# Causal attention on one core: scores of two steps, then products of the preceding two

## The chip, the cores and the metric

The kernel runs on one core of a Trainium2 chip. Its engines work side by side, each through a queue of its own in program order, and meet only at semaphores: TensorE (PE, matrix products into the eight banks of PSUM), VectorE (DVE), ScalarE (ACT), GpSimd (POOL), and the DMA queues, of which this kernel uses SyncE's (SP). The metric is the device time of one execution in microseconds (us); less is better.

## The reference, cut to what matters

The whole model is two layers, each a token mixer and a feed-forward part, on 2 sequences of 1024 tokens with 512 channels. The change lies in the attention of the second layer, which has 16 heads of 32 channels:

```python
qkv = x @ qkv_w.T + qkv_b
q, k = _rope(q), _rope(k)
scores = jnp.einsum('bhqd,bhkd->bhqk', q, k) / np.sqrt(D)
scores = jnp.where(causal, scores, -jnp.inf)
attn = jax.nn.softmax(scores, axis=-1)
out = jnp.einsum('bhqk,bhkd->bqhd', attn, v).reshape(b, t, c)
return out @ out_w.T + out_b
```

## The kernel before, in words

`attend` (L1858) works through 8 units; a unit is 4 heads of one sequence. For each unit there are `NS` = 12 steps. A step (`STEPS`, L1865) is one pair of a block of 512 queries (`qc`) and a tile of 128 keys (`j`): steps 0 to 3 belong to the first block of queries, steps 4 to 11 to the second. Steps 0 to 3 and 8 to 11 lie on the diagonal; there the columns left of it are left out, so that their widths are 512, 384, 256 and 128 columns. Steps 4 to 7 are 512 wide.

For one step, for each of 4 heads, TensorE computes the transposed scores (`scores`, L2039, 98 rows of the array by 128 columns) into one of `ST` = 3 PSUM banks `st`; ScalarE takes the exponential out of the bank into `pt` (`exps`, L2009); GpSimd masks the diagonal (L1991). Then TensorE multiplies `pt` by the values into `num` and by ones into `den` (`pv`, L2058: eight matmuls a step, four beside each other, each in 32 columns of the array). `num` and `den` are one bank each, and gather over all steps of one block of queries; after the last step of a block (`ENDS`: 3 and 11) they are copied out, and DVE inverts the denominators in 4 chunks (`invert`, L2084) and multiplies (L2087); SP stores the result.

The softmax needs each query's maximum. `Maxima` computes it one unit ahead: 48 score pieces per unit (`piece`, L1372, up to 512 columns, three PSUM banks `mx` in turn), each reduced by DVE (`top`: L1384 with the mask, or L1387). The pieces of a head come in groups of four, with widths 128, 256, 384, 512; 512, 128, 512, 256; 512, 384, 512, 512. `pieces_at` says which pieces stand with which step: they are put between the step's four score matmuls. With `LAST_PIECES` = 8 and `FRONT` = 12, steps 0 to 8 carry 36 pieces (4 each) of the next unit and steps 10 and 11 carry 12 pieces (6 each) of the one after it. At `TURN_STEP` = 9 the maxima are joined (L1392), transposed by TensorE (L1397), negated by ACT (L1402) and DVE (L1407), and sent by SP as two more rows of the queries. The third piece that follows waits for that negation, since it writes the bank of the transpose.

The order is written out by hand, in one loop for each engine. TensorE issues the scores of step g (with pieces), then `pv` of step g - 2 (`LAG` = 2); `pt` has `PT` = 3 buffers. ACT issues the exponentials of step g and, where step g - 2 ended a block, then the copies of `den` and `num` (`copy_out`, L2000 and L2001). DVE issues the pieces of step g, and after them one chunk of inversion at steps 2 to 5 (second block of the unit before) and 7 to 10 (first block of this unit). The last unit (7) has no pieces; there ACT also splits the attention output of earlier units into high parts (`out.high`, L1811, two tiles at each of steps 6 to 9) and DVE into low parts. At step 4 of each unit GpSimd's queue has three casts of expert weights (`narrow`, L2175), which wait for their loads by SP's queue; the loads stand behind those of the next queries and keys, which wait for the last `pv` of the unit before.

## Time and profile before

| | us |
|---|---|
| median of 3 runs | 1529.63 |
| lowest and highest of these | 1527.41 and 1530.99 |
| span of the profiled execution (first to last instruction) | 1527.3 |
| TensorE busy in it | 1465.1 (96%) |
| VectorE busy | 976.4 (64%) |
| ScalarE busy | 614.1 (40%) |
| GpSimd busy | 472.3 (31%) |
| attention, first score matmul to the first matmul of the output projection | 905.91 to 1245.68 |

The page names only the span for the profiled execution; the runs' median lies 2.3 us above it. Busy times of TensorE overlap: matmuls are pipelined, and the end of each is modelled, so that gaps on TensorE are read from the starts of its rows. "Idle before" in a row of the timeline is the engine's idle time, with what ended it.

### The profile page before, as it was taken

Reading aid. Unit: us, or ns where it says so; the run is one execution under the profiler, and the core shown is the slowest. Engines: PE = TensorE matmul, PEld = TensorE weight load, DVE = VectorE, ACT = ScalarE, POOL = GpSimd, SP = SyncE. Lnnn points to the kernel's source line nnn. Section 1 sums busy time; section 2 is a strip of 40 time slices with the busy share of each in tenths; the row PEclk is TensorE's granted clock in tenths of the full one; section 3 lists DMA queues with packets and bytes.
Section 4 is the critical chain, followed back from the end, with each engine's and each line's share of the span. In section 5 each row is a group of like instructions: output and inputs, shape, how many; then the busy total and the mean of one; then the engine's idle time right before and its main releaser. Section 6 shows DMA issues by size and latency. Waiting matters only on the chain. (4 is left out here: it accounts for less than half of the span.)

```text
span 1527.3 us, 22410 instructions
## 1 busy us (share of the span) xinstructions
PE 1465.1 (96%) x7681; PEld 1072.6 (70%) x7696; DVE 976.4 (64%) x1897; ACT 614.1 (40%) x1079; POOL 472.3 (31%) x391
## 2 busy tenths in 40 slices
PE   7999989999999999999999999999999999999987
PEld 5788778788888888888888774444444458777554
DVE  6888987854545554454233666778787557667664
ACT  4343455613421441342121124555554546432544
POOL 1233334303420440241152231211223237103773
PEclk9999999999999999999999989999999999999999
DMA  6121347504320430334256685666556445853336
GB/s 215 34 71 65 152 166 248 180 14 138 96 69 29 151 96 27 110 96 149 82 191 192 207 244 138 192 198 155 155 173 213 150 152 218 303 208 132 105 101 238
DMA packets 105228, 223.38 MB, mean 146 GB/s; under 512 B 9328, under 2 KB 35312, under 8 KB 104240
## 3 DMA queue, kind: packets, MB, share of 16 engines
q1 hardware_dynamic: 101392, 211.96, 42.8%
q0 software_dynamic: 3744, 10.23, 2.2%
q8 instruction: 54, 0.88, 0.2%
q14 instruction: 38, 0.31, 0.1%
HBM read 157.54 MB, written 64.36 MB: 145 GB/s over the span
## 5 line engine op out<-in xcount | busy, mean ns | idle before, releaser
L2009 ACT ACTIVATE at_pt<-at_st 128x512 f32<-128x512 f32 (+3 forms) x384 | 164.1, 499 | 147.4 <-PE at_st L2039 146.5
L969 POOL TENSOR_TENSOR ff_w_lo<-ff_raw,ff_w_hi 128x1024 fp32r<-128x1024 f32 x64 | 153.7, 2402 | 220.8 <-ACT ff_w_hi L999 206.6
L115 PE MATMUL op_bank<-ff_x_hi,ff_w_lo 128*128 128x512 f32 x512 | 199.9, 390 | 0.2 <-issue 0.2
L116 PE MATMUL op_bank<-ff_x_lo,ff_w_hi 128*128 128x512 f32 x512 | 199.6, 390 | 0.0
L117 PE MATMUL op_bank<-ff_x_hi,ff_w_hi 128*128 128x512 f32 x512 | 199.5, 390 | 0.0
L1239 DVE TENSOR_TENSOR ff_h_lo<-ff_hf,ff_h_hi 128x512 f32 (+1 forms) x64 | 146.8, 2293 | 53.9 <-ACT ff_h_hi L1127 53.6
L999 ACT ACTIVATE ff_w_hi<-ff_raw 128x1024 fp32r<-128x1024 f32 x64 | 67.9, 1063 | 118.3 <-PE op_bank L117 116.0
L2039 PE MATMUL at_st<-mx_qp,mx_kp 98*128 98x512 f32 (+3 forms) x288 | 103.0, 390 | 12.6 <-ACT at_pt L2009 9.5
L1384 DVE CUSTOM_DVE_ANT_0 mx_mx<-mx_mx,mx_mask 128x128 f32<-128x128 f32 (+2 forms) x200 | 101.5, 517 | 21.1 <-PE mx_mx L1372 20.0
L115 PEld LDWEIGHTS op_bank<-ff_x_hi,ff_w_lo 128*128 128x128 f32 x512 | 96.4, 188 | 20.7 <-issue 0.6
L117 PEld LDWEIGHTS op_bank<-ff_x_hi,ff_w_hi 128*128 128x128 f32 x512 | 96.4, 188 | 20.4
L116 PEld LDWEIGHTS op_bank<-ff_x_lo,ff_w_hi 128*128 128x128 f32 x512 | 96.4, 188 | 20.1
L2039 PEld LDWEIGHTS at_st<-mx_qp,mx_kp 98*128 98x128 f32 x288 | 54.3, 195 | 69.7 <-issue 33.4
L115 PE MATMUL mx_mx<-ff_down_hi,ff_h_lo 128*128 128x512 f32 x256 | 100.2, 391 | 0.0
L116 PE MATMUL mx_mx<-ff_down_lo,ff_h_hi 128*128 128x512 f32 x256 | 99.7, 389 | 0.0
L117 PE MATMUL mx_mx<-ff_down_hi,ff_h_hi 128*128 128x512 f32 x256 | 99.7, 389 | 0.0
L1231 DVE SCALAR_TENSOR_TENSOR ff_hf<-op_bank,ff_sc,ff_hf 128x512 f32<-128x512 f32 x64 | 48.0, 750 | 72.3 <-PE op_bank L117 71.6
L1991 POOL TENSOR_SCALAR_AFFINE_SELECT at_pt<-at_pt 128x512 f32<-128x512 f32 x64 | 41.1, 646 | 149.9 <-ACT at_pt L2009 149.8
L1372 PE MATMUL mx_mx<-mx_kp,mx_qp 96*128 96x512 f32 (+1 forms) x208 | 75.9, 371 | 6.7 <-DVE mx_tops L1384 2.9
L2058 PE MATMUL at_den<-at_pt,at_ones 128*32 128x512 f32 (+3 forms) x768 | 82.2, 500 | 0.0
L1120 ACT ACTIVATE ff_hf<-op_bank,ff_sc 128x512 f32<-128x512 f32 x64 | 44.2, 690 | 82.6 <-PE op_bank L117 82.6
L1565 POOL TENSOR_TENSOR qkv_part_lo<-qkv_whole,qkv_part_hi 128x512 fp32r<-128x512 f32 x32 | 42.6, 1332 | 88.3 <-ACT qkv_part_hi L1580 80.8
(467 smaller groups left out, 3333.4 us busy)
## 6 DMA issues: line engine op xcount, KB each, us to landing
ff_raw<-in_Wug SPq DMA_DIRECT2D x64, 512.0 KB, 3.6
at_raw<-in_expert_gu SPq DMA_DIRECT2D x16, 704.0 KB, 12.1
mx_qp<-q_hi SPq DMA_DIRECT2D x12, 512.0 KB, 6.5
mx_kp<-k_hi SPq DMA_DIRECT2D x12, 512.0 KB, 11.6
at_raw<-in_expert_d SPq DMA_DIRECT2D x8, 768.0 KB, 13.7
expert_gu_bf<-at_cast SPq DMA_DIRECT2D x16, 352.0 KB, 10.9
ex_e_gu<-expert_gu_bf SPq DMA_DIRECT2D x8, 704.0 KB, 8.3
tm_ln_res<-in_x SPq DMA_DIRECT2D x4, 1024.0 KB, 5.5
```

The source lines that it names most:

```text
L115: pe.matmul(out, cut_l(ll), cut_r(rh), start=first, stop=False, **kw)
L116: pe.matmul(out, cut_l(lh), cut_r(rl), start=False, stop=False, **kw)
L117: return pe.matmul(out, cut_l(lh), cut_r(rh), start=False, stop=last, **kw)
L969: pool.tensor_tensor(w[j][1][:, :, :, :], raw[:, j], f32(w[j][0][:, :, :, :]), ALU.subtract)\
L999: act.activation(w[j][0][:, :, :, :], raw[:, j], ACT.Copy).then_inc(w_hi_ready, 1)
L1231: dve.scalar_tensor_tensor(hf[:, j, :], up[j][:, :], sc[:, UP, bass.ds(n + j, 1)], hf[:, j, :], ALU.mult, ALU.mult).then_inc(hf_ready, 1)
L1239: dve.tensor_tensor(h_lo[:, bass.ds(n + j, 1), :], hf[:, j:j + 1, :], f32(h_hi[:, bass.ds(n + j, 1), :]), ALU.subtract).then_inc(h_lo_read ...
L1372: pe.matmul(bank[:, 0:hi - lo], self.qp[j][0:R_MAX, h, qt * P:(qt + 1) * P], self.kp[j][0:R_MAX, h, lo:hi], start=True, stop=True).then_in ...
L1384: dve.tensor_tensor_reduce(piece, piece, self.mask[:, TB - (hi - lo):], 1.0, -3e38, ALU.add, ALU.max, out)\
L2009: act.activation(pt[:, s % PT, h, off:TB], st[(s * HG + h) % ST][:, off:TB], ACT.Exp, scale=SCALE).then_inc(exp_done, 1)
L2039: pe.matmul(st[(s * HG + h) % ST][:, off:TB], kp[j][0:ROWS, h, kt * P:(kt + 1) * P], qp[j][0:ROWS, h, qc * TB + off:(qc + 1) * TB], start= ...
L2058: mm = pe.matmul(total[rows, off:TB], vv[u % SLOTS][:, kt, rows] if lhs is None else lhs[:, :], pt[:, s % PT, h, off:TB], start=first, sto ...
```

## The change

The loops of TensorE, ACT and DVE go by pairs of steps (`PAIR` = 2). TensorE issues the scores of two steps with their pieces, then `pv` of the two steps before. `pt` has 4 buffers in place of 3. The pieces are spread anew: `TURN_STEP` = 9 is now also the last step of the first stretch and `FRONT` is 8, so that every step of a middle unit carries 4 pieces. ACT copies the denominators only, behind the exponentials of the next pair; DVE copies the numerators (`copy_num`), behind its pieces and inversions of that pair. DVE inverts two chunks in a pair: in the pairs (2, 3) and (4, 5) for the unit before, in (6, 7) and (8, 9) for this unit. ACT waits at the start for the stores of the values by the stage before (`v_stored`), and DVE does in unit 0 before pair (2, 3). `last_at`, where later rows of the residual lie, moves by one buffer.

```diff
@@ -1865,20 +1865,19 @@
     STEPS = [(qc, j) for qc in range(QC) for j in range((qc + 1) * TT)]
     NS = len(STEPS)
     DIAGS = sum(j >= qc * TT for qc, j in STEPS)
-    LAST_PIECES, TURN_STEP, FRONT = 8, 9, 12
-    LAG = 2
-    PT = LAG + 1
+    PAIR = 2
+    TURN_STEP, FRONT = 9, 8
+    PT = 2 * PAIR
     ST = 3
     DIVIDE_CHUNKS = 4
     CHUNK = TB // DIVIDE_CHUNKS
-    DIVIDE_LAST, DIVIDE_FIRST = 2, 7
     OW_STEP, SPLITS = 1, {6: [(0, (0, 1))], 7: [(0, (2, 3))], 8: [(1, (0, 1))], 9: [(1, (2, 3))]}
-    assert NS % PT == 0 and NS * HG % ST == 0 and NP % 3 == 0 and QC == 2 and (UNITS - 2) % SLOTS == 0
+    assert NS % PAIR == 0 and NS * HG % ST == 0 and NP % 3 == 0 and QC == 2 and (UNITS - 2) % SLOTS == 0
     with Bench(nc, "at_") as b:
         mx.add_slot(b)
         qp, kp, vv = mx.qp, mx.kp, mx.vv
         pt = b.sb("pt", [P, PT, HG, TB])
-        last_at = b.next_at() - 2 * TT * C * 4
+        last_at = b.next_at() - 3 * TT * C * 4
         num_sb, den_sb = b.sb("num_sb", [P, QC, TB]), b.sb("den_sb", [P, QC, TB])
         ones = b.sb("ones", [P, HD])
         st = [b.psum(f"st{s}", [P, TB]) for s in range(ST)]
@@ -1910,20 +1909,27 @@
 
         def pieces_at(u, s):
 
-            if s <= LAST_PIECES:
+            if s <= TURN_STEP:
                 begin = FRONT if u else 0
                 count = NP - begin
-                lo, hi = (begin + count * n // (LAST_PIECES + 1) for n in (s, s + 1))
+                lo, hi = (begin + count * n // (TURN_STEP + 1) for n in (s, s + 1))
                 return [(u + 1, n) for n in range(lo, hi)] if u + 1 < UNITS else []
-            if s <= TURN_STEP or u + 2 >= UNITS:
+            if u + 2 >= UNITS:
                 return []
             after = NS - 1 - TURN_STEP
             lo, hi = (FRONT * n // after for n in (s - TURN_STEP - 1, s - TURN_STEP))
             return [(u + 2, n) for n in range(lo, hi)]
 
-        def place(g):
-
-            return g // NS, g % NS
+        def pairs():
+
+            return [(u, [s, s + 1]) for u in range(UNITS) for s in range(0, NS, PAIR)]
+
+        def ended_before(u, steps):
+
+            s = steps[0] - 1
+            if s in ENDS:
+                return u, ENDS.index(s)
+            return (u - 1, QC - 1) if s < 0 and u else None
 
         @block.sync
         def _(sp):
@@ -1994,33 +2000,34 @@
 
         @block.scalar
         def _(act):
-            def copy_out(u, qc):
+            def copy_den(u, qc):
                 act.wait_ge(pv_done, u * NS + ENDS[qc] + 1)
                 at_least(act, o_stored[qc], u * DMA)
                 act.activation(den_sb[:, qc, :], den[:, :], ACT.Copy).then_inc(copied, 1)
-                act.activation(num_sb[:, qc, :], num[:, :], ACT.Copy).then_inc(copied, 1)
 
             def exps(u, s):
                 off = diag(s) or 0
 
-                at_least(act, pv_done, u * NS + s - LAG)
+                at_least(act, pv_done, u * NS + s - PT + 1)
                 for h in range(HG):
                     act.wait_ge(scores_done, (u * NS + s) * HG + h + 1)
                     act.activation(pt[:, s % PT, h, off:TB], st[(s * HG + h) % ST][:, off:TB], ACT.Exp,
                                    scale=SCALE).then_inc(exp_done, 1)
 
-            for g in range(UNITS * NS):
-                u, s = place(g)
-                exps(u, s)
-                if g >= LAG and place(g - LAG)[1] in ENDS:
-                    ended, at = place(g - LAG)
-                    copy_out(ended, ENDS.index(at))
-                if s == TURN_STEP and u + 1 < UNITS:
+            for stored in mx.v_stored:
+                act.wait_ge(stored, NB * TT // 2 * DMA)
+            for u, steps in pairs():
+                for s in steps:
+                    exps(u, s)
+                    if u == UNITS - 1:
+                        for i, ks in SPLITS.get(s, ()):
+                            out.high(act, i, ks, pv_done)
+                ended = ended_before(u, steps)
+                if ended:
+                    copy_den(*ended)
+                if TURN_STEP in steps and u + 1 < UNITS:
                     mx.negate_high(act, u + 1)
-                if u == UNITS - 1:
-                    for i, ks in SPLITS.get(s, ()):
-                        out.high(act, i, ks, pv_done)
-            copy_out(UNITS - 1, QC - 1)
+            copy_den(UNITS - 1, QC - 1)
             out.high(act, 2, range(KT), pv_done)
             out.scale(act, 0)
             out.high(act, 3, range(KT), pv_done)
@@ -2060,18 +2067,21 @@
                 mm.then_inc(pv_done, 1)
 
             pe.wait_ge(ones_small_set, 1)
-            for g in range(UNITS * NS):
-                u, s = place(g)
-                if s == 0:
+            before = None
+            for u, steps in pairs():
+                if steps[0] == 0:
                     pe.wait_ge(mx.ones_set, min(u + 1, SLOTS))
                     pe.wait_ge(mx.rows_loaded, (u + 1) * 2 * DMA)
-                scores(u, s)
-                if g >= LAG:
-                    pv(*place(g - LAG))
-                if s == TURN_STEP and u + 1 < UNITS:
+                for s in steps:
+                    scores(u, s)
+                if before:
+                    for s in before[1]:
+                        pv(before[0], s)
+                if TURN_STEP in steps and u + 1 < UNITS:
                     mx.turn(pe, u + 1)
-            for g in range(UNITS * NS - LAG, UNITS * NS):
-                pv(*place(g))
+                before = u, steps
+            for s in before[1]:
+                pv(before[0], s)
             for i in range(NB - 1):
                 out.project(pe, i)
             expert_tensor(pe)
@@ -2086,23 +2096,43 @@
                     dve.wait_ge(inverted, (u * QC + qc + 1) * DIVIDE_CHUNKS)
                     dve.tensor_tensor(num_sb[:, qc, :], num_sb[:, qc, :], den_sb[:, qc, :], ALU.mult).then_inc(divided, 1)
 
-            for g in range(UNITS * NS):
-                u, s = place(g)
-                for of, n in pieces_at(u, s):
-                    mx.top(dve, of, n)
-                if s == LAST_PIECES and u + 1 < UNITS:
+            def copy_num(u, qc):
+                dve.wait_ge(pv_done, u * NS + ENDS[qc] + 1)
+                at_least(dve, o_stored[qc], u * DMA)
+                dve.tensor_copy(num_sb[:, qc, :], num[:, :]).then_inc(copied, 1)
+
+            for u, steps in pairs():
+                if u == 0 and steps[0] == PAIR:
+                    for stored in mx.v_stored:
+                        dve.wait_ge(stored, NB * TT // 2 * DMA)
+                for s in steps:
+                    for of, n in pieces_at(u, s):
+                        mx.top(dve, of, n)
+                    if u == UNITS - 1:
+                        if s == OW_STEP:
+                            ow.low(dve)
+                        for i, ks in SPLITS.get(s, ()):
+                            out.low(dve, i, ks)
+                if TURN_STEP in steps and u + 1 < UNITS:
                     mx.join(dve, u + 1)
-                if s == TURN_STEP and u + 1 < UNITS:
+                if u and steps[0] == PAIR:
+                    invert(u - 1, 1, 0)
+                    invert(u - 1, 1, 1)
+                if u and steps[0] == 2 * PAIR:
+                    invert(u - 1, 1, 2)
+                    invert(u - 1, 1, 3)
+                if steps[0] == 3 * PAIR:
+                    invert(u, 0, 0)
+                    invert(u, 0, 1)
+                if steps[0] == 4 * PAIR:
+                    invert(u, 0, 2)
+                    invert(u, 0, 3)
+                ended = ended_before(u, steps)
+                if ended:
+                    copy_num(*ended)
+                if TURN_STEP in steps and u + 1 < UNITS:
                     mx.negate_low(dve, u + 1)
-                if u and 0 <= s - DIVIDE_LAST < DIVIDE_CHUNKS:
-                    invert(u - 1, 1, s - DIVIDE_LAST)
-                if u == UNITS - 1:
-                    if s == OW_STEP:
-                        ow.low(dve)
-                    for i, ks in SPLITS.get(s, ()):
-                        out.low(dve, i, ks)
-                if 0 <= s - DIVIDE_FIRST < DIVIDE_CHUNKS:
-                    invert(u, 0, s - DIVIDE_FIRST)
+            copy_num(UNITS - 1, QC - 1)
             for chunk in range(DIVIDE_CHUNKS):
                 invert(UNITS - 1, 1, chunk)
             out.add(dve, 0)
```

## Rows read from the trace of the kernel before

**Rows 1.** The page: its first line.
```profile
span 1527.3 us, 22410 instructions
```
**Rows 2.** Windows: us, busy (x count) of PE, PEld, DVE, ACT, POOL, PEclk, DMA share, GB/s.
```profile
990.00:995.00 5.00, 4.87 (x22) 1.80 (x23) 3.91 (x13) 0.43 (x3) 1.35 (x3) 0.68 0.06 20
```
**Rows 3.** TensorE's timeline, steps 7 and 8 of a unit: start, duration, engine, line, operation.
```profile
1064.84 0.40 PE L2039 MATMUL at_st<-mx_qp,mx_kp 98*128 98x512 f32 x1
1065.08 0.28 PE L1372 MATMUL at_mx<-mx_kp,mx_qp 96*128 96x256 f32 x1
1065.29 1.06 PE L2058 MATMUL at_num<-at_pt,mx_vv 128*32 128x512 f32 x8
1066.17 1.04 PE L2058 MATMUL at_den<-at_pt,at_ones 128*32 128x512 f32 x8
1067.14 0.50 PE L2039 MATMUL at_st<-mx_qp,mx_kp 98*128 98x512 f32 x1
1067.48 0.40 PE L1372 MATMUL mx_mx<-mx_kp,mx_qp 96*128 96x512 f32 x1
```
**Rows 4.** TensorE's timeline: first scores of steps 7, 10, 0, 2, 4, 6, 7.
```profile
1063.44 0.50 PE L2039 MATMUL at_st<-mx_qp,mx_kp 98*128 98x512 f32 x1
...
1074.37 0.36 PE L2039 MATMUL at_st<-mx_qp,mx_kp 98*128 98x256 f32 x1
...
1083.68 0.50 PE L2039 MATMUL at_st<-mx_qp,mx_kp 98*128 98x512 f32 x1
...
1088.95 0.38 PE L2039 MATMUL at_st<-mx_qp,mx_kp 98*128 98x256 f32 x1
...
1095.64 0.50 PE L2039 MATMUL at_st<-mx_qp,mx_kp 98*128 98x512 f32 x1
...
1101.06 0.50 PE L2039 MATMUL at_st<-mx_qp,mx_kp 98*128 98x512 f32 x1
...
1105.80 0.50 PE L2039 MATMUL at_st<-mx_qp,mx_kp 98*128 98x512 f32 x1
```
**Rows 5.** TensorE's timeline: pieces 3 and 4 of step 10.
```profile
1075.33 0.41 PE L1372 MATMUL mx_mx<-at_kp,at_qp 96*128 96x384 f32 x1 [0.24 <-issue]
...
1076.39 0.50 PE L1372 MATMUL mx_mx<-at_kp,at_qp 96*128 96x512 f32 x1 [0.54 <-DVE mx_tops L1384]
```
**Rows 6.** DVE's timeline: pieces, an inversion, the product.
```profile
1064.83 0.29 DVE L1384 CUSTOM_DVE_ANT_0 mx_mx<-mx_mx,mx_mask 128x128 f32<-128x128 f32 x1
...
1065.99 0.95 DVE L2084 RECIPROCAL at_den_sb<-at_den_sb 128x128 f32<-128x128 f32 x1
1067.92 0.69 DVE L1387 TENSOR_REDUCE mx_tops<-mx_mx 128x1 f32<-128x512 f32 x1 [0.98 <-PE mx_mx L1372]
1068.53 0.56 DVE L1384 CUSTOM_DVE_ANT_0 mx_mx<-mx_mx,mx_mask 128x384 f32<-128x384 f32 x1
...
1102.51 0.69 DVE L2087 TENSOR_TENSOR at_num_sb<-at_num_sb,at_den_sb 128x512 f32<-128x512 f32 x1
```
**Rows 7.** ACT's timeline: four exponentials; the denominators' copy; two splits of the last unit.
```profile
1064.04 2.07 ACT L2009 ACTIVATE at_pt<-at_st 128x512 f32<-128x512 f32 x4 [2.16 <-PE at_st L2039]
...
1089.08 0.60 ACT L2000 ACTIVATE at_den_sb<-at_den 128x512 f32<-128x512 f32 x1 [0.30 <-PE at_den L2058]
...
1231.01 1.17 ACT L1811 ACTIVATE at_o_hi<-at_raw_o 128x512 fp32r<-128x512 f32 x2
```
**Rows 8.** GpSimd's timeline: the last cast of a unit and the first masks behind it.
```profile
1074.43 1.47 POOL L2175 CAST at_cast<-at_raw 128x1536 bf16<-128x1536 f32 x1 [1.40 <-DMA at_raw<-in_expert_d]
1075.85 1.22 POOL L1991 TENSOR_SCALAR_AFFINE_SELECT at_pt<-at_pt 128x512 f32<-128x512 f32 x2
```
**Rows 9.** SP's timeline: its first load of the stage, behind its wait for the values' stores.
```profile
905.91 0.38 SPq L1715 DMA_DIRECT2D ow_raw<-in_outT  x1
```
**Rows 10.** TensorE's timeline: step 0 of the last unit, which has no pieces.
```profile
1208.46 0.96 PE L2039 MATMUL at_st<-mx_qp,mx_kp 98*128 98x512 f32 x3
1209.71 0.50 PE L2039 MATMUL at_st<-mx_qp,mx_kp 98*128 98x512 f32 x1 [0.29 <-ACT at_pt L2009]
```

## The prediction, made before the change was run

> **What bounds the kernel now.** I read the page's engines and slices first: TensorE is busy nearly everywhere, so the question is what its time in the attention is made of. Then TensorE's timeline of one unit, from start to start, since the ends of pipelined matmuls are modelled; then the timelines of DVE, ACT, GpSimd and SP over the same unit, to see which of them each gap waits for; last the granted clock by stretches of 5 us. The span is 1527.3 us [rows 1], and a unit in the middle takes 1105.80 - 1063.44 = 42.36 us [rows 4].
>
> Three things fill a unit. First the matmuls: within a stretch of scores and pieces a 512-column matmul follows the other after 0.24 us, a product of a step (eight matmuls, four at a time) takes 0.88 us for `num` and as much for `den` [rows 3]. Second the switch between the two kinds. The 256-column piece at 1065.08 should take half of 0.24 and the product starts 0.21 later: 0.09 lost. From `den` to the next score there are 0.97 instead of 0.88 (0.09), and from that score to the next matmul 0.34 instead of 0.24 (0.10) [rows 3]. That is 0.28 us for each step, whoever waits for whom. Third the waits for DVE and ACT: in step 10, piece 3 comes 0.96 us after the first score (the negation), and piece 4 stands idle 0.54 us for DVE [rows 4, 5]. TensorE is on the path throughout; ACT and DVE reach it through the three banks each that they must empty.
>
> **The change part by part.** *Switches.* One for two steps instead of one for each: 6 of 12 go, 6 x 0.28 = 1.7 us a unit, 13 us over 8 units. No other engine covers them, so this gain is sure; the question is how much of it waits give back.
>
> *The stretch of scores in a pair.* It holds 8 scores and 8 pieces. TensorE alone would need 8 x 0.24 for 512-wide scores, 0.6 to 0.9 us for each four pieces (by their columns), and 0.19 for the switch. Two limits stand against that. Score k waits for exponential k - 3: the first exponential starts 0.60 after the first score and takes 0.6, and four take 2.07, one in 0.5 [rows 3, 4, 7]; so the fourth score comes at 1.25 (as 1209.71 - 1208.46 in the unit without pieces [rows 10]) and the eighth at 1.25 + 4 x 0.52 = 3.3. Piece k waits until DVE has read piece k - 3. DVE starts 0.44 after a 512-column piece (1067.92 against 1067.48 [rows 3, 6]) and goes on every 0.61 for 512 columns (1067.92 to 1068.53), and by duration less 0.08 every 0.48 for 384 and 0.21 for 128, about 0.34 for 256 [rows 6]: 1.7, 1.8 and 2.3 us for the three groups of four. A read is visible to TensorE some 0.2 us after the next one begins, my estimate from such rows.
>
> *DVE's other work.* An inversion takes 0.95, or 0.82 until the next can start (estimate: 0.95 less the overlap that pieces show), the product 0.69 [rows 6]. New is the copy of 128x512 from PSUM: no row shows it; the nearest, the reduction of a bank, is 0.69 (next start 0.61), ACT's copy of such a bank 0.60 [rows 6, 7]. I take 0.61 and 0.5 to 1.0 as bounds. ACT in turn loses a copy of such a size, twice a unit; it was not on the path except behind the end of a block. The VectorE: DVE Perf Modes page of the Trainium skill (Specifications) puts VectorE nearer to SBUF and ScalarE nearer to PSUM, which speaks against moving a PSUM copy to DVE; the two rows differ by 0.09 us, so by them it is worth 0.2 us a unit at most.
>
> *Pair by pair, middle units* (before, from [rows 4]; after = scores stretch + products of the pair before, 0.09 less for their inner border; products in proportion to columns):
> - (0, 1): before 5.27. DVE's eight reads run from 0.78; piece 7 needs the read of piece 4 at 3.5; stretch 4.08, products 1.41: 5.49.
> - (2, 3): before 6.69. The narrow scores leave TensorE little to do, and DVE copies the numerators until 0.74 first; piece 7 waits until 3.28; stretch 3.71, products 3.17: 6.88.
> - (4, 5): before 5.42. The eighth score, at 3.3, decides; 3.75 + 1.41 = 5.16. DVE is through with its pieces at 4.4, but has two inversions and the product (2.4) still, and only then the copy.
> - (6, 7): before 4.74 + 3.70 = 8.44 (steps 7 and 8 from the unit before). That copy ends 2.2 us after the pair begins, with three pieces waiting in their banks: piece 3 comes at 3.0 instead of 1.4; stretch 5.57, products 3.61: 9.18.
> - (8, 9): before 7.23. DVE is free again; 3.83 + 3.67 (with the transpose) = 7.50.
> - (10, 11): before 9.31, with 12 pieces, two inversions and a product on DVE between them. Now 8 pieces and nothing else; the negation still holds piece 3 until 0.96. Stretch 3.6, products 3.17: 6.77.
>
> The sum is 40.98: 1.38 less than 42.36. Five units (1 to 5) give -6.9. Unit 6 prepares no unit after it, so it has no pieces in (10, 11) before or after; without that pair it loses, 34.2 against 33.05: +1.2. Unit 0 has no inversions of a unit before it, so that its pairs keep up; it gains the 2.5 us of (10, 11) and five switches, 1.4: -3.9, with 2 us either way, as its pieces are spread differently. Unit 7 has no pieces, and a pair of 512-wide steps needs 3.3 + 0.43 for its scores against 2 x 1.68 before; the two splits in ACT's queue between exponentials (1.17 for two [rows 7]) now hold the eighth score in pairs (6, 7) and (8, 9), by 0.7 and 1.4: +2.4 in all.
>
> *Waits added, and moved queues.* ACT's wait for the values' stores comes first in its queue, ahead of all exponentials; SP waits for the same semaphores and had its load out at 905.91 [rows 9], before the first score ended: 0 us, and 0.5 if it is seen later. DVE's stands behind the pieces of a whole pair: 0. The fourth `pt` buffer lets exponentials run two steps ahead; only products free it, earlier than needed. SP's loads hang on the last product of the unit before, which moves with the unit. GpSimd's casts end at 1075.9 [rows 8]. The last product before that unit's loads ended about 1046.7 (the next unit's is done by 1089.08 [rows 7], and a unit takes 42.36): 29.2 us. Masks 8 and 9 follow 0.6 and 1.2 us later: 35.4 us after the unit's start. The first product that needs mask 8 starts at 37.8, so the casts are hidden by some 2.4 us; they are a floor if everything else goes better. The end of the stage moves as a whole: the projection that follows starts on blocks loaded long before.
>
> Sum: -6.9 - 3.9 + 1.2 + 2.4 = -7.2 us. The profiled execution would have a span of 1520.1; the median stands 2.3 us above the span of before, so 1522.4.
>
> **The rivals.**
> *A, DVE keeps up.* The waits of (2, 3) and (6, 7) are smaller than drawn (1.2 and 2.0 us above what TensorE needs), for instance as reads are seen earlier. Then the casts become the floor: 2.4 us less in each of units 1 to 5, 1510. For it: DVE is idle for a fifth of the new unit (4 x 5.8 for pieces, 8 x 0.82, 2 x 1.3, some 33 us of 41). Against it: the copy is bound to the last product, whatever its size.
>
> *B, the clock.* In 990 to 995 the granted clock was 0.68 [rows 2], a part of that stretch at 1.2 instead of 2.4 GHz; it cost 0.32 x 5 = 1.6 us, and the timeline shows the like once more in a later unit, at the same place: behind step 10, whose waits are those of rows 5, in two units of seven. The new stretch of (6, 7) idles 2.0 us of 5.57, and (10, 11) 1.4 of 3.6. If the clock fell once in each of units 0 to 6, that were 5 x 1.6 = 8 us more: 1530. The page TensorE: Matmul & The Clock Gate of the Trainium skill (Why this matters for your kernels) says that idle gaps between bursts of matmuls bring the clock down; by it alone waits as short as those drawn keep the clock, and the sum stays 1522, while by the row it can fall behind several waits of 0.54 us at most.
>
> *C, waits that take turns (slower).* A matmul after a wait is followed only 0.34 us later, as after a switch (rows 3; 0.10 each time). If in each pair the scores wait for ACT and the pieces for DVE alternately, 10 of 16 matmuls pay that, some 0.6 us a pair more than I counted, 3.6 a unit in units 0 to 6 at most: 1548; at half of it, 1535. From 0.2 us a pair on the gain is gone. For it: both limits lie within 0.3 us of each other in (0, 1), (4, 5) and (8, 9). Against it: three banks on each side let one wait cover the other.
>
> *D, the switch stays.* If the 0.28 us belong to the first matmuls behind a semaphore and not to the change of kind, then pairs save none of it: +13, 1536. Against it: inside a product, from `num` to `den`, nothing is lost.
>
> **How the numbers follow.** Forecast 0.47 (its own range 1515 to 1529), A 0.15, B 0.16, C 0.16, D 0.06. A measurement of this kernel can tell 0.2%, 3.1 us, from no change. Faster by more: most of the forecast and A, 0.57. Within: B and the forecast's upper edge, 0.21. Slower: C and D, 0.22. For 8 in 10 the range runs from A to the half of C, with 2 us on either side: 1508 to 1537.
>
> **What would show it.** A middle unit of 41 us, with (10, 11) shortest against before (6.8 for 9.3) and (6, 7) longer (9.2 for 8.4), its fourth piece waiting for DVE behind a numerators' copy that starts 1.6 us late. One switch of 0.28 a pair. In unit 7, the eighth scores of (6, 7) and (8, 9) waiting for ACT behind a split. Wrong would be: products that wait for masks (A's floor), a clock under 1.0 in more than two units (B), or waits for ACT and DVE alternating through a stretch (C).

## The result, and the profile after

The median rose from 1529.73 to 1533.41 us (16 runs each; one of before took 4622.33 us, and without it before's median is 1529.63): a ratio of 1.0026, with a 95% interval of 1.0017 to 1.0036. The kernel became slower by a quarter of a per cent, where the prediction had 1522.4 and "faster" as the likeliest; its range, 1508 to 1537, held the time.

The page of after, its first line, the engines' busy times and the granted clock by slices of the span (before: [rows 1]):

```profile
span 1531.1 us, 22440 instructions
...
PE 1473.1 (96%) x7696; PEld 1079.4 (70%) x7696; DVE 983.6 (64%) x1913; ACT 603.6 (39%) x1063; POOL 474.7 (31%) x391
...
PEclk9999999999999999999999989999999999999999
```

In tenths of full speed the clock looks the same as before. As a mean over the span it is 0.980, and before it was 0.989. Over the runs of after the time goes with this mean: 1528.56 us at 0.984, 1533.29 at 0.980, 1538.38 at 0.978.

By windows of 5 us the loss has places. Columns as in [rows 2]; these are the ends of pair (10, 11) of unit 1 and of pair (6, 7) of unit 3:

```profile
985.00:990.00 5.00, 4.57 (x23) 2.38 (x27) 3.70 (x15) 1.58 (x6) 2.28 (x4) 0.76 0.17 61
990.00:995.00 5.00, 5.00 (x35) 2.48 (x27) 1.59 (x4) 1.77 (x4) 0.00 (x0) 0.90 0.00 0
...
1055.00:1060.00 5.00, 3.81 (x15) 2.45 (x14) 4.90 (x13) 3.87 (x8) 0.00 (x0) 0.93 1.05 213
1060.00:1065.00 5.00, 5.00 (x35) 1.25 (x33) 3.00 (x6) 0.63 (x2) 0.00 (x0) 0.73 1.06 399
```

The last column but two is the granted clock. Each window's length times what its clock lacks to 1, summed from 905 to 1250, is 22.1 us after against 10.3 before. The first 15 us of the stage hold 5.1 (after) and 6.8 (before) of it; the rest is 17.0 against 3.5. The span grew by 3.8, which less the clock's 11.8 leaves -8.0. That is near the forecast of -7.2, and the clock took it back. The sum is rough: it prices every window as if TensorE's clock alone set its length.

A "fall" is a stretch of time at the lower clock. How one looks on TensorE, in pair (6, 7) of unit 3 (start, duration, engine, line, operation, idle before):

```profile
1054.63 0.50 PE L2046 MATMUL at_st<-mx_qp,mx_kp 98*128 98x512 f32 x1
...
1056.09 0.39 PE L2046 MATMUL at_st<-mx_qp,mx_kp 98*128 98x512 f32 x1
1057.62 0.50 PE L1372 MATMUL mx_mx<-mx_kp,mx_qp 96*128 96x512 f32 x1 [1.14 <-DVE mx_tops L1387]
...
1059.36 0.69 PE L1372 MATMUL mx_mx<-mx_kp,mx_qp 96*128 96x384 f32 x1
...
1060.83 1.94 PE L2065 MATMUL at_num<-at_pt,mx_vv 128*32 128x512 f32 x8
1062.54 1.10 PE L2065 MATMUL at_den<-at_pt,at_ones 128*32 128x512 f32 x8
```

The pair begins at 1054.63; piece 3 is next behind the score of 1056.09, and TensorE stands idle for 1.14 us before it. From about 1059.4 matmuls take 0.63 to 0.69 instead of 0.34 to 0.40, and a product of eight starts 1.71 before the next instead of 0.88 [rows 3]: TensorE is at 1.2 GHz until 1062.5. What piece 3 waited for stands in DVE's timeline:

```profile
1053.88 1.76 DVE L2094 RECIPROCAL at_den_sb<-at_den_sb 128x128 f32<-128x128 f32 x2
1055.67 0.69 DVE L2097 TENSOR_TENSOR at_num_sb<-at_num_sb,at_den_sb 128x512 f32<-128x512 f32 x1
1056.28 0.68 DVE L2102 COPY at_num_sb<-at_num 128x512 f32<-128x512 f32 x1
1056.88 0.68 DVE L1387 TENSOR_REDUCE mx_tops<-mx_mx 128x1 f32<-128x512 f32 x1
```

Two inversions, the product and the new copy of pair (4, 5) run until 2.25 us after pair (6, 7) has begun; only then, at 1056.88, does DVE read the first of three full banks.

A second thing was in no step of the prediction. In unit 1, at the border of pairs (8, 9) and (10, 11):

```profile
982.92 1.47 POOL L2205 CAST at_cast<-at_raw 128x1536 bf16<-128x1536 f32 x1 [1.43 <-DMA at_raw<-in_expert_d]
983.26 1.66 DVE L2097 TENSOR_TENSOR at_num_sb<-at_num_sb,at_den_sb 128x512 f32<-128x512 f32 x1
...
984.85 0.27 DVE L1407 SCALAR_TENSOR_TENSOR mx_neg_lo<-mx_mx,mx_neg_hi 32x128 fp32r<-32x128 f32 x1
...
985.22 0.41 PE L1372 MATMUL mx_mx<-mx_kp,mx_qp 96*128 96x384 f32 x1 [0.66 <-issue]
```

DVE's product takes 1.66 us instead of 0.69 [rows 6], and ends half a microsecond behind GpSimd's cast. The negation stands behind it, and piece 3 comes 1.49 us after the pair's first score (983.73), where 0.96 was counted. (10, 11) has 4.32 and 4.37 for 3.60 in the two units with the longest products, 1 and 5. Before, that product came 3.5 to 3.8 us after the end of the third cast, and in units 0 to 6 all products took 0.69.

In unit 2, where (10, 11) took longest (4.58), the same cast met another operation of DVE, the join of the maxima; the last row is the join of unit 3, which met none:

```profile
1025.73 1.47 POOL L2205 CAST at_cast<-at_raw 128x1536 bf16<-128x1536 f32 x1 [1.43 <-DMA at_raw<-in_expert_d]
1025.81 1.42 DVE L1392 TENSOR_TENSOR mx_tops<-mx_tops 128x16 f32<-128x16 f32 x1
...
1070.29 0.17 DVE L1392 TENSOR_TENSOR mx_tops<-mx_tops 128x16 f32<-128x16 f32 x1
```

The inversions, the product and the negation stand behind the join, and piece 3 of unit 2 comes 1.75 us after the pair's first score.

The lengths of the units in us, from first score to first score of (0, 1), unit 7 to the first matmul of the projection, before and after: unit 0 49.16 and 44.73; units 1 to 5 together 214.80 and 216.68; unit 6 38.59 and 40.91; unit 7 37.22 and 41.45.

### The profile page after: what moved, and what is told of

Its sections match the earlier page's. It is cut to its first block and busy times, and to the rows that moved or that the text cites. A ratio compares the mean times of both kernels' runs of the same rounds, so it can differ in the third digit from the quotient of the medians.

```text
span 1531.1 us, 22440 instructions
## 1 busy us (share of the span) xinstructions
PE 1473.1 (96%) x7696; PEld 1079.4 (70%) x7696; DVE 983.6 (64%) x1913; ACT 603.6 (39%) x1063; POOL 474.7 (31%) x391
## 5 line engine op out<-in xcount | busy, mean ns | idle before, releaser
L2205 POOL CAST at_cast<-at_raw 128x1408 bf16<-128x1408 f32 (+1 forms) x24 | 33.4, 1394 | 123.4 <-DMA at_raw<-in_expert_gu 114.4
```

## The experiments

"After" is the changed kernel. Stretches are from first score to first product, products from there to the next score, in us. Medians are of four to ten runs; rows, stretches and falls are those of the one profiled execution of each kernel.

**The inversions one pair later.** DVE's inversions of the pairs (4, 5), (6, 7) and (8, 9), and the products behind them, are moved one pair on in units 0 to 6; nothing else.

```diff
+                late = PAIR if u + 1 < UNITS else 0
-                if u and steps[0] == 2 * PAIR:
+                if u and steps[0] == 2 * PAIR + late:
                     invert(u - 1, 1, 2) ...
-                if steps[0] == 3 * PAIR:
+                if steps[0] == 3 * PAIR + late:
                     invert(u, 0, 0) ...
-                if steps[0] == 4 * PAIR:
+                if steps[0] == 4 * PAIR + late:
                     invert(u, 0, 2) ...
```

> The changed kernel with the inversions of units 0 to 6 moved by one pair: those of pair (4, 5) to (6, 7), those of (6, 7) to (8, 9), those of (8, 9) to (10, 11), where DVE had nothing beside pieces; unit 7 as before the move. Theory: DVE is through with the pieces of (4, 5) before the products end, so its copy starts at once, and the first piece of (6, 7) is read at 0.75 us instead of 2.2: the stretch takes 4.1 instead of 5.55 to 6.2 us, with no wait long enough to bring the clock down; 1.5 to 2 us a unit for the wait and some 1.2 for the clock: 1510 to 1518. Rival (the order in pairs as such lets the clock fall): the stretch shrinks, the products after it still run at half clock in about each unit: 1522 to 1525.

Measured 1512.03 us, ratio to before 0.9886 (0.9864 to 0.9908): faster than both kernels. Pair (6, 7) of unit 3 now, on TensorE and DVE:

```profile
1047.07 0.50 PE L2046 MATMUL at_st<-mx_qp,mx_kp 98*128 98x512 f32 x1
...
1048.51 0.40 PE L2046 MATMUL at_st<-mx_qp,mx_kp 98*128 98x512 f32 x1
1048.75 0.40 PE L1372 MATMUL mx_mx<-mx_kp,mx_qp 96*128 96x512 f32 x1
...
1051.16 1.07 PE L2065 MATMUL at_num<-at_pt,mx_vv 128*32 128x512 f32 x8
...
1047.20 0.69 DVE L2102 COPY at_num_sb<-at_num 128x512 f32<-128x512 f32 x1 [0.74 <-PE at_den L2065]
```

The copy starts 0.13 after the pair (1047.07), as soon as the denominators' last matmul ends, and piece 3 stands nowhere. The stretch is 4.09 instead of 5.5 to 6.2, the units 1 to 5 are 39.21 to 39.24 long, and in them the clock never falls. The casts no longer meet a product (all 0.69 in units 0 to 6). This one edit takes away the wait of (6, 7) and the meeting with the cast together; the next runs take them one by one.

**Matmuls in place of the wait.** In after, the fourth score matmul of step 6 is issued seven times in units 1 to 6, where piece 3 would wait. It adds work and takes no wait away.

```diff
+                    if s == 3 * PAIR and h == HG - 1 and 0 < u < UNITS - 1:
+                        for _ in range(6):
+                            pe.matmul(st[(s * HG + h) % ST][:, off:TB], ...)
                     pe.matmul(st[(s * HG + h) % ST][:, off:TB], ...)
```

> The changed kernel, in which TensorE fills its wait for DVE in pair (6, 7) of units 1 to 6: the fourth score matmul of step 6 is issued seven times instead of once, with the same result each time (1.4 us more matmuls in a wait of 1.1 to 1.6 us). Nothing else changes. Theory (the clock falls because TensorE idles in that stretch): the stretch keeps its 5.55 us, since DVE sets it, the clock stays up behind it, and the products take 3.57 instead of 4.4 to 4.8 us: 4 to 8 us less than the changed kernel, 1526 to 1529, although work was added. Rival (the clock falls for something else, such as the kind of matmul or the time since the last fall): falls stay, and the time is the same or up to 3 us longer, 1533 to 1537.

Measured 1526.31, 0.9992 of before (0.9976 to 1.0008): 7 us less than after by the medians, 5 by the ratios to before. Unit 3:

```profile
1053.35 1.54 PE L2048 MATMUL at_st<-mx_qp,mx_kp 98*128 98x512 f32 x6
...
1054.96 0.44 PE L1372 MATMUL mx_mx<-mx_kp,mx_qp 96*128 96x512 f32 x1
...
1057.48 1.06 PE L2069 MATMUL at_num<-at_pt,mx_vv 128*32 128x512 f32 x8
```

Piece 3 comes 3.06 us after the pair began (1051.90), as late as without the fill (2.99), and the stretch is 5.55 to 5.58; but in units 1 to 6 the products behind it take 3.57 throughout, where four of the six had 4.46 to 4.84. Piece 3 comes no earlier, so what (6, 7) gained came from the clock alone. It is not the whole gain. Units 1 to 5 are 10.0 us shorter together, 4.7 of it at (6, 7) and 5.3 at (10, 11), which the fill does not touch: one fall there in place of four. Why is not shown.

**The last product away from the cast.** In after, only DVE's fourth inversion of the first block and its product go from pair (8, 9) to (10, 11), behind the negation.

```diff
                 if steps[0] == 4 * PAIR:
                     invert(u, 0, 2)
-                    invert(u, 0, 3)
+                if steps[0] == 5 * PAIR:
+                    invert(u, 0, 3)
```

> The kernel after, with one thing moved: DVE's last inversion of the first block and the product behind it, from the pair (8, 9) to the pair (10, 11), behind the negation. In the trace of after that product took 1.66, 1.14 and 1.71 us in units 1, 3 and 5 where it overlapped GpSimd's third cast of 1.47 us, against 0.69 without such an overlap, and the negation stands behind it. Theory (two causes, this one and the wait in (6, 7)): the product is 0.69 again, the stretch (10, 11) 3.6 in all units where it was up to 4.58, so -2.5 us over the units, and the clock no longer falls behind (10, 11), where products took 4.42 to 4.84 for 3.14 in four units, -6.1; (6, 7) stays at 5.5 with its own falls: 1523 to 1528. Rival 1 (the overlap costs nothing on the path): 1531 to 1535. Rival 2 (the product is all that the kernel with later inversions gained by): 1510 to 1515.

Measured 1522.64, ratio 0.9953 (0.9936 to 0.9970), a little under the theory of two causes. The cast's row, the negation and piece 3, and further on the product:

```profile
984.38 1.47 POOL L2206 CAST at_cast<-at_raw 128x1536 bf16<-128x1536 f32 x1 [1.44 <-DMA at_raw<-in_expert_d]
...
985.72 0.28 DVE L1407 SCALAR_TENSOR_TENSOR mx_neg_lo<-mx_mx,mx_neg_hi 32x128 fp32r<-32x128 f32 x1 [1.89 <-ACT mx_neg_hi L1402]
986.10 0.41 PE L1372 MATMUL mx_mx<-mx_kp,mx_qp 96*128 96x384 f32 x1
...
990.42 0.69 DVE L2097 TENSOR_TENSOR at_num_sb<-at_num_sb,at_den_sb 128x512 f32<-128x512 f32 x1
```

Piece 3 comes 0.96 after the first score (985.14), (10, 11) takes 3.60 in all units, and three units measure 40.66 to 40.71. One point was not expected: (6, 7) still takes 5.55, yet its products are slow in one unit of six, not four. Of the 9.9 us that units 1 to 5 gain, 6.9 come at (10, 11) and 3.1 at (6, 7). And the clock falls once behind a (10, 11) of 3.60.

**ACT copies again.** After, with the numerators' copies back on ACT.

```diff
                 act.activation(den_sb[:, qc, :], den[:, :], ACT.Copy).then_inc(copied, 1)
+                act.activation(num_sb[:, qc, :], num[:, :], ACT.Copy).then_inc(copied, 1)
...
-                if ended:
-                    copy_num(*ended)
```

> The changed kernel with one part undone: ACT copies the numerators again, behind the denominators; the pairs, the spread of pieces and the places of the inversions stay. Theory (the clock falls behind the stretch of scores of pair (6, 7), in which TensorE waits for DVE, whose queue is late by two inversions, the product and the copy): DVE starts the pieces of (6, 7) 0.6 us earlier, so that stretch shrinks from 5.55 or more to about 4.95 us in units 1 to 6, and the clock falls more seldom there, but not never: 3 to 8 us less than the changed kernel, 1526 to 1530. Rival (the copy on DVE is the whole trouble): the stretch comes down to some 4.2 us and the clock stays up, 1518 or less. Rival (the clock falls for the order in pairs as such): the stretch shrinks, but the clock falls as often: 4 us less, 1529.

Measured 1531.09, ratio 1.0023 (1.0003 to 1.0043), with 10 runs from 1525.25 to 1540.85: no clear gain, and above the theory's 1526 to 1530. The trace, of a run of 1528.14, says why: (6, 7) shrinks from 5.54 to 4.96 and its products are fast in units 1 to 6, but DVE, early by the copy's time, now meets the cast with its product in each of the units 1 to 5:

```profile
1026.76 1.47 POOL L2202 CAST at_cast<-at_raw 128x1536 bf16<-128x1536 f32 x1 [1.43 <-DMA at_raw<-in_expert_d]
1027.07 1.70 DVE L2098 TENSOR_TENSOR at_num_sb<-at_num_sb,at_den_sb 128x512 f32<-128x512 f32 x1
...
1029.07 0.41 PE L1372 MATMUL mx_mx<-mx_kp,mx_qp 96*128 96x384 f32 x1 [1.06 <-issue]
```

(10, 11) takes 4.54 to 5.07 for it. TensorE stands idle there for 1.06 to 1.59 us in one piece, and yet the products behind are slow in one unit of the five only (4.84 for 3.14).

**DVE's copies alone.** The kernel before, with nothing of the change but the numerators' copies on DVE, behind its inversion of the step.

```diff
-                act.activation(num_sb[:, qc, :], num[:, :], ACT.Copy).then_inc(copied, 1)
...
                     invert(u, 0, s - DIVIDE_FIRST)
+                if g >= LAG and place(g - LAG)[1] in ENDS:
+                    ended, at = place(g - LAG)
+                    copy_num(ended, ENDS.index(at))
```

> The kernel before with one part of the change alone: DVE copies the numerators, behind the pieces and the inversion of the step; ACT copies the denominators only. Order by single steps, as before. Theory (DVE is the engine that is late at step 6): the stretch of step 6, which waits for DVE before the change, grows by some 0.6 us in units 0 to 6, and ACT's exponentials of steps 2 and 6 start 0.5 us earlier for 0.3 us of gain at step 2: +2 to +5 us, 1532 to 1535, with the clock falling no more often than before. Rival (the copy is hidden on DVE): 1528 to 1530.

Measured 1535.68, ratio 1.0054 (1.0037 to 1.0070), a little over the theory's upper end. Step 6 of unit 3:

```profile
1060.56 0.68 DVE L2091 COPY at_num_sb<-at_num 128x512 f32<-128x512 f32 x1
...
1061.56 0.60 PE L1372 MATMUL mx_mx<-mx_kp,mx_qp 96*128 96x512 f32 x1 [1.29 <-DVE mx_tops L1384]
...
1062.09 1.94 PE L2057 MATMUL at_num<-at_pt,mx_vv 128*32 128x512 f32 x8
```

Behind an inversion and a product, the copy makes TensorE wait 1.29 us in one piece; step 6 has 3.6 for 2.9, and its products take 3.37 for 1.85 in five of the units 1 to 6. Unit 3 becomes 44.39 for 42.39 long, three quarters of that by the clock. The theory had the clock fall no more often than before; that part of it failed.

**The new spread alone.** The kernel before, with four pieces at each step and none in groups of six.

```diff
-    LAST_PIECES, TURN_STEP, FRONT = 8, 9, 12
+    LAST_PIECES, TURN_STEP, FRONT = 9, 9, 8
```

> The kernel before, with the new spread of pieces alone (four with each of the steps 0 to 9 and 10, 11, none in groups of six); no pairs, copies by ACT. Theory: the gain forecast for (10, 11) belongs to the spread and not to the pairs: eight pieces there for twelve, 4 x 0.53 us less for DVE, which is on the path there, and four pieces more in step 9, +0.6; -1.5 us in each of six units: 1518 to 1522. Rival (the spread needs the pairs: step 9's pieces now hold the transpose and the negation up by as much): 1527 to 1532.

Measured 1521.71, ratio 0.9944 (0.9923 to 0.9964). Units 2 and 3 are 41.07 and 41.12 long, 1.27 less; steps 10 and 11 with their products have 7.44 for 9.31, and step 9's scores 1.89 for 1.46. No pair is needed for this part. In units 1, 4 and 5 the join meets the third cast and takes 1.42, 1.27 and 1.42, TensorE waits for it, and step 9's products last 2.66 to 2.81 for 1.89: the spread alone can bring about this collision.

**Pairs on TensorE alone.** The kernel with later inversions, TensorE going by single steps again.

```diff
-                for s in steps:
-                    scores(u, s)
-                if before:
-                    for s in before[1]:
-                        pv(before[0], s)
+                for n, s in enumerate(steps):
+                    scores(u, s)
+                    if before:
+                        pv(before[0], before[1][n])
```

> The kernel with later inversions (1512.0), with all as it is on the other engines, but TensorE going by single steps again: scores of one step, products of one step. It undoes the part of the change that the prediction called a sure gain. Theory 1 (the prediction's): six switches of 0.28 us come back in each unit and nothing else changes, 8 x 1.7 = +13 us: 1525. Theory 2 (the switches saved were paid back by waits in the doubled stretch at once): the rows of before for steps with four pieces sum to 5.27 + 6.71 + 5.43 + 7.22 = 24.63 us for (0, 1), (2, 3), (4, 5), (8, 9), and the kernel with later inversions has 5.47 + 6.80 + 5.19 + 7.34 = 24.80 for the same: 1508 to 1515.

Measured 1518.36, ratio 0.9922 (0.9905 to 0.9939), between the two theories. A switch and its rows, to be held against [rows 3]:

```profile
1082.54 0.38 PE L1372 MATMUL at_mx<-at_kp,at_qp 96*128 96x256 f32 x1
1082.85 1.06 PE L2065 MATMUL at_num<-at_pt,mx_vv 128*32 128x512 f32 x8
1083.73 1.04 PE L2065 MATMUL at_den<-at_pt,at_ones 128*32 128x512 f32 x8
1084.70 0.33 PE L2046 MATMUL at_st<-mx_qp,mx_kp 98*128 98x128 f32 x1
```

Again 0.97 from `den` to the next score. Units 1 to 5 are 41.35 to 41.38 long against 39.21 to 39.24: 2.14 us for six switches, 0.80 of it in the products, the rest in the scores with their waits, among them one of 0.56 for DVE in step 0. The total rose by 6.3 only, since unit 7 loses its wait for the splits (next run) and the clock lost less at the start of the stage (5.1 us for 7.5; below).

**The splits behind both exponentials.** The kernel with later inversions; in unit 7 ACT's splits follow the pair's eight exponentials.

```diff
                 for s in steps:
                     exps(u, s)
+                for s in steps:
                     if u == UNITS - 1:
                         for i, ks in SPLITS.get(s, ()):
```

> The kernel with later inversions (1512.0), and in the last unit ACT's splits behind both exponentials of a pair instead of between them. Theory: the eighth score waits for ACT no longer; (6, 7) 4.99 to 3.7, (8, 9) 4.50 to 3.7, and the products behind (6, 7) 6.36 to 3.57 as the clock stays: -4.9 us, 1507. Rival (ACT's time comes back in the next pair, whose exponentials then wait behind two splits): 1511 to 1513.

Measured 1506.83, ratio 0.9853 (0.9837 to 0.9870), the best of all. In after, pair (6, 7) of unit 7 has a split on ACT between exponentials, and the eighth score behind it:

```profile
1225.40 1.18 ACT L1811 ACTIVATE at_o_hi<-at_raw_o 128x512 fp32r<-128x512 f32 x2
...
1227.12 0.80 PE L2046 MATMUL at_st<-mx_qp,mx_kp 98*128 98x512 f32 x1 [1.01 <-ACT at_pt L2014]
```

Here eight exponentials run in one go, and the split follows beside the products:

```profile
1202.03 4.02 ACT L2014 ACTIVATE at_pt<-at_st 128x512 f32<-128x512 f32 x8
...
1202.67 2.46 PE L2047 MATMUL at_st<-mx_qp,mx_kp 98*128 98x512 f32 x5 [0.31 <-ACT at_pt L2014]
...
1205.84 0.72 ACT L1811 ACTIVATE at_o_hi<-at_raw_o 128x512 fp32r<-128x512 f32 x1
```

(6, 7) takes 3.67 for 4.99 and (8, 9) 3.47 for 4.50. The clock still falls behind (6, 7), where scores wait up to 0.31 us for ACT; the products have 5.24 for 6.37, where the theory had 3.57. The stretches went as the theory said; that the median met it (1507) is in part luck.

**ACT copies in the balanced kernel.** The run above, with the edit of "ACT copies again".

> The best kernel so far (1506.8), with ACT copying the numerators again: it undoes DVE's copies where DVE's work is spread evenly. Theory (a copy costs little on either engine where neither is late; the copy by DVE hurt only behind the inversions of (4, 5)): 1505 to 1509, with stretches that move by 0.2 us at most. Rival 1 (DVE is the limit still, and each copy by it costs 0.6 us): 2 x 0.6 us in each of seven units less, 1498 to 1500. Rival 2 (ACT's copies hold up the exponentials of the next pair): 1510 to 1515.

Measured 1510.99, ratio 0.9884 (0.9867 to 0.9902): slower by 4 us than with DVE's copies, outside the theory and in the range of the second rival. In unit 3 the exponentials of (6, 7) start 1.10 us after its first score instead of 0.64, behind ACT's two copies, and the fourth score waits for them, as that rival had it. (6, 7) has 4.38 to 4.40 for 4.09 in units 1 to 6 and 4.16 for 3.67 in unit 7, whose (2, 3) has 2.84 for 2.35, with a fall behind it; the other stretches of units 1 to 6 stay within 0.02. Here, where DVE is not late, its copy is the cheaper one.

**The clock at the start of the stage.** Ahead of the first score TensorE idles 3.1 us in every kernel so far, and the granted clock of 905 to 910 is 0.50 to 0.70 behind that. From 910 to 920 it differs: 0.50 with the splits behind, 0.75 and 0.66 in after, 0.96 and 1.00 with ACT's copies in the balanced kernel. So the "about 0.5 for 15 us" that the next expectation gives for every kernel is wrong. To the kernel with the splits behind, twelve matmuls are added before the attention's first wait:

```diff
+            for _ in range(12):
+                pe.matmul(mx.bank[1][:, :], mx.qp[0][0:R_MAX, 0, 0:P], mx.kp[0][0:R_MAX, 0, 0:TB], ...)
             pe.wait_ge(ones_small_set, 1)
```

> The best kernel so far (later inversions and splits behind, 1506.8), and before the attention's first wait twelve matmuls of 512 columns more into a bank that nothing reads, in the 3.1 us in which TensorE waits there for GpSimd's ones. In every kernel so far that wait is followed by a granted clock of about 0.5 for 15 us (905 to 920). Nothing else changes and work is added, so this tests the clock alone. Theory (an idle TensorE brings the clock down, and the lower clock costs what the rows at either level say): the first two stretches of scores take about 4.0 + 3.7 for 11.8 and the first products 3.14 for 5.2, -6 us: 1500 to 1502; with the clock kept only in part, 1503 to 1505. Rival (the first stretches are bound by DVE and ACT at either clock, or the clock falls for another reason): 1506 to 1509.

Measured 1512.10, ratio 0.9902 (0.9879 to 0.9925): a miss, by the experiment's fault. The idle time is that of a barrier between two stages, and the twelve ran behind it, not in it:

```profile
904.70 4.57 PE L2071 MATMUL mx_mx<-mx_kp,mx_qp 96*128 96x512 f32 x12 [2.95 <-PEq L87]
909.11 0.40 PE L2047 MATMUL at_st<-mx_qp,mx_kp 98*128 98x512 f32 x1
```

So eleven of them were put at the end of the stage before, ahead of the barrier.

> The same fill as in the run before, in its right place. There the twelve matmuls came behind the barrier between the stages (their rows begin at 904.70, the first score at 909.11 instead of 905.73), so that TensorE idled as before and they stood on the path. Here eleven of them end the stage of the projections, ahead of the barrier, in the 3.1 us that TensorE idles there; the rest is the kernel of 1506.8. Theory (the idle time ahead brings the clock down): a granted clock near 1.0 from 905 to 920 instead of 0.5, stretches of 7.7 for 11.8 and products of 3.14 for 5.2, -6 us: 1500 to 1502; kept in part: 1503 to 1505. Rival (the clock falls there for another reason, or the first stretches are bound by DVE and ACT at either clock): 1506 to 1509.

Measured 1506.99, ratio 0.9854 (0.9835 to 0.9874): as fast as without, as the rival had it. Windows from 905 on, first without, then with the fill:

```profile
905.00:910.00 5.00, 4.27 (x13) 3.70 (x13) 2.46 (x9) 2.83 (x5) 4.22 (x3) 0.50 0.64 203
910.00:915.00 5.00, 4.98 (x18) 4.38 (x17) 4.67 (x15) 3.28 (x8) 1.16 (x3) 0.50 0.95 222
915.00:920.00 5.00, 5.00 (x20) 2.42 (x23) 3.11 (x10) 0.83 (x3) 0.81 (x2) 0.50 1.02 213
```

```profile
905.00:910.00 5.00, 3.29 (x16) 2.11 (x14) 2.40 (x9) 2.42 (x6) 3.17 (x2) 1.00 0.46 127
910.00:915.00 5.00, 4.57 (x21) 2.94 (x19) 5.00 (x19) 3.53 (x11) 2.39 (x4) 1.00 0.90 256
915.00:920.00 5.00, 4.68 (x27) 1.41 (x30) 1.95 (x6) 0.29 (x2) 0.64 (x1) 0.66 1.03 210
```

The clock stays up for 10 us. In no kernel with the idle time is it above 0.70 from 905 to 910, so there the idle time goes with the low clock; for the second window this proves little, since 0.96 was seen without any fill. But the stage begins 1.2 us later, the first stretches still take 9.1 for 11.8, with DVE busy 5.00 of 5.00 in the second window, and the clock falls at 915. Of the 6 us expected the span shows 1.6, the median nothing.

## Why the prediction failed

**The pair table was right.** In us, the stretch and the products behind it; "clean" is what after shows where the clock stays up and DVE meets no cast:

| pair | predicted | clean in after | later inversions |
|---|---|---|---|
| (0, 1) | 4.08 + 1.41 | 4.04 + 1.44 | 4.04 + 1.44 |
| (2, 3) | 3.71 + 3.17 | 3.67 + 3.14 | 3.66 + 3.14 |
| (4, 5) | 3.75 + 1.41 | 3.75 + 1.44 | 3.75 + 1.44 |
| (6, 7) | 5.57 + 3.61 | 5.54 + 3.57 | 4.09 + 3.57 |
| (8, 9) | 3.83 + 3.67 | 3.74 + 3.61 | 3.73 + 3.61 |
| (10, 11) | 3.60 + 3.17 | 3.60 + 3.14 | 3.60 + 3.14 |

The clean unit is 40.67 against a forecast of 40.98. DVE's copy took 0.68 (the next start 0.60), where 0.61 was taken; DVE was free for the pieces of (6, 7) 2.25 us after the pair began (2.2 forecast), and piece 3 came at 2.99 (3.0).

**The step that failed is the sum's clock.** The forecast let the clock be as it was, that is with before's two falls (units 1 and 5, 43.88 and 43.85 long for 42.36), and put nothing for falls behind the waits that the change adds. The mechanism stood in the text, as rival B, with a chance of 0.16 and a price of 8 us, one fall in each of units 0 to 6. In units 1 to 5 after lost 13.3 us against clean units: 9.2 in products at the lower clock, 4.1 in longer stretches of (6, 7) and (10, 11), of which casts hold a part. The clock fell seven times there, in two units twice, once more in unit 6 and once in unit 7, where the rival had none. The stage became 4.0 us longer, not 7.2 shorter; of these 11.2 us, units 1 to 5 hold 8.8, units 6 and 7 hold 2.9, and unit 0 was 0.5 better than forecast. The tally of TensorE's longest idle time in a stretch, and of how often the products behind were slow:

- step 6, copies alone: 1.27 to 1.30 us, five of units 1 to 6;
- (6, 7), after: 1.14, four of six;
- (6, 7), product later: 1.12 to 1.15, one of six;
- (6, 7), filled with matmuls: 0.05 at most, none;
- (6, 7), later inversions: 0.02 at most, none;
- (10, 11), ACT copies again: 1.06 to 1.59, one of units 1 to 5.

So idle time counts, as the fill in (6, 7) shows, but the length of one wait doesn't decide. The page TensorE: Matmul & The Clock Gate of the Trainium skill (Why this matters for your kernels) says that idle gaps between bursts of matmuls bring the clock down, and the fill agrees; the prediction read from it that waits as short as these keep the clock, and that does not hold here. The mistake was one of weight: [rows 2] showed a fall behind step 10, whose longest idle time in [rows 5] is 0.54 us, the table drew 2.0 us of idle time into (6, 7), and the text still left B a sixth of the chance.

**A collision no step held.** That "the casts are hidden by some 2.4 us" was worked out for the masks behind them. What the casts do to DVE was not asked, though the change moves DVE's product from step 10 to the end of (8, 9), where the third cast runs. In units 1 and 5 it met the cast and 0.69 became 1.66 and 1.71; in unit 3 it met the mask behind the cast, 1.14, and piece 3 was not late; in unit 2 the join met the cast, 1.42 for 0.17. The run that moves that product alone gives 10.8 us back, not all of it the collision's own price: three falls behind (6, 7) went too. In after, DVE's inversions, with one input in SBUF, take 0.91 beside a cast and 0.92 elsewhere, and the reductions, which read PSUM, 0.69 both ways; the product and the join, each with two inputs in SBUF, take up to 1.0 and 1.25 longer. The Trainium skill, SBUF — State Buffer (SBUF: two separate sides), has the rule: a VectorE operation with two inputs in SBUF and a GpSimd operation that reads SBUF lock one pair of ports against each other for the whole instruction. The rows agree with it. That the port is the cause is the page's word; the runs show the overlap and its price.

**Switches.** 1.7 us a unit "is sure": 2.14 measured, with (6, 7) cured, of which 0.56 is a wait for DVE in step 0 that stands there only when TensorE alone goes by single steps. Rival D is out, since the products, in which no wait falls, hold 0.80 of it. Rival C too: no clean stretch is longer than the table drew it.

**(10, 11)** gains 2.57 of a forecast 2.54, but 1.87 of it belong to the spread of pieces, which the kernel before can have without pairs, for 0.43 more in step 9.

**Units 0, 6 and 7.** Unit 0 gained 4.43 (3.9 forecast), though the clock of its first 15 us, which was in no step, lost 1.7 less than before: the nearness is in part luck. Unit 6 lost 2.32 (1.2) and unit 7 4.23 (2.4), each with a fall. The splits themselves cost 2.3 us in unit 7's two stretches (2.1 forecast).

**Waits at the start** for the values' stores: 0 as forecast; the first exponential starts 0.62 after the first score (0.53 before).

What stays open: why the same wait (1.12 to 1.15 us) is followed by the lower clock in four units of six in one kernel and in one of six in another, and longer waits mostly by none; why a cure at one of the two pairs made falls rarer at the other too; and what brought the clock down behind (10, 11) of unit 3, whose stretch took 3.61, as in units without a fall.

## What to carry to other kernels

A wait of TensorE has two prices: its length, and the matmuls at half speed that may follow; where rows of the kernel show one such fall, count with the second price at every wait of that size that the change makes, and spread the other engine's work so that no wait stands in one piece. When an operation of DVE with two inputs in SBUF is moved, however short it is, look at what GpSimd runs at its new place. A sum that is right stretch by stretch can still have the wrong sign if all stretches are priced at one clock.

## What the runs showed of the hardware

- Behind single waits of 1.14 us (after) and 1.27 to 1.30 us (copies alone) TensorE's granted clock fell from 2.4 to 1.2 GHz in four and five units of six; behind waits of 1.06 to 1.59 us in another place (ACT copies again) in one of five. With the wait of (6, 7) filled by matmuls there was no fall.
- From run to run of after the time follows the mean clock: 9.8 us between runs at 0.984 and at 0.978.
- A DVE product of two SBUF tensors of 128x512 takes up to 1.72 us beside a GpSimd cast of 1.47 (ACT copies again), alone 0.69. A DVE maximum of two tensors of 128x16 takes 1.42 beside one (after), alone 0.17.
- Going from products in 32 columns to scores in 128 and back costs 0.36 us a time with the waits that came with it (2.14 for six, pairs on TensorE alone).
